# Packing of a gated delta-rule attention kernel: two sequences per partition set with quarter-array products, in place of three sequences with whole-array products

## What is computed

```python
h = tok(x)                                   # 16 x 37 x 256
q, k, v = silu(causal_conv4(h @ Wq)), ...    # 8 heads, key 128, value 64
q, k = l2norm(q), l2norm(k)
beta = 2 * sigmoid(h @ Wb); alpha = exp(-exp(A_log) * softplus(h @ Wa + dt_bias))
state = alpha * (state - beta * (state k) k^T) + beta * v k^T     # for each token
o = state q
o = o * rsqrt(mean(o^2) + 1e-5) * o_norm_w * silu(h @ Wg)
h = layernorm(h + o @ Wo)
h = layernorm(h + int8_linear(h) + bias)
```

## Time and profile before

| | us |
|---|---|
| median of 3 runs | 252.26 |
| profiled execution, span from first to last instruction | 249.4 |
| PE busy | 212.5 (85%) |
| weight loads busy | 175.9 (71%) |
| DVE busy | 183.3 (73%) |
| ACT busy | 91.5 (37%) |
| POOL busy | 57.5 (23%) |

### The profile page before, as it was taken

How to read it: one execution, slowest core, us unless ns; L and a number is a source line. 1 busy time by engine, 2 the same in 40 slices (tenths; PEclk the granted TensorE clock), 3 DMA queues, 4 the chain that set the end, 5 groups by cost and what they waited for, 6 DMA issues and landing times.

```text
span 249.4 us, 3855 instructions
## 1 busy us (share of the span) xinstructions
PE 212.5 (85%) x1292; PEld 175.9 (71%) x1292; DVE 183.3 (73%) x393; ACT 91.5 (37%) x168; POOL 57.5 (23%) x65
## 2 busy tenths in 40 slices
PE   8999897929978999999699999777989999995430
PEld 3767566917856899797489979566868989983320
DVE  0136358999789969799995979989999851355692
ACT  2017883343261554224645422340621123103911
POOL 9100002330000033306003330600260080043541
PEclk9999798895997999989999999977999999999655
DMA  6991110010010001001000000000000000000004
GB/s 222 362 353 47 42 63 0 1 45 0 1 50 13 3 0 45 1 0 42 24 0 0 0 0 0 0 0 0 0 1 4 0 3 0 3 0 1 0 0 106
DMA packets 5682, 8.93 MB, mean 36 GB/s; under 512 B 1251, under 2 KB 3299, under 8 KB 5539
## 3 DMA queue, kind: packets, MB, share of 16 engines
q1 hardware_dynamic: 5075, 8.65, 10.6%
q10 hardware_dynamic: 592, 0.10, 0.3%
HBM read 8.09 MB, written 0.66 MB: 35 GB/s over the span
## 4 chain that ended last, share of the span: by engine, by line
PE 60%; DVE 22%; issue 9%; POOL 3%; ACT 2%; DVEq 1%; POOLq 0%; ACTq 0%
PE PYV L1349 13%; PE PA L1218 12%; PE PS L1311 8%; PE PS L1334 6%; DVE conv L722 5%; PE PA L1197 2%; PE PS L1197 2%; PE PA L1374 2%; DVE tmp L862 2%; PE PYV L1287 2%; DVE xg L804 2%; PE PR L1374 2%; DVE tri L867 1%; POOL x_sb L444 1%; DVE EMs L813 1%
## 5 line engine op out<-in xcount | busy, mean ns | idle before, releaser
L722 DVE SCALAR_TENSOR_TENSOR conv<-xp,tap_sb,conv 128x640 f32<-128x640 f32 x60 | 55.6, 938 | 8.3 <-ACT conv L483 6.7
L402 POOL TENSOR_TENSOR EMs<-Xf,cst 120x640 f32<-120x640 f32 x8 | 15.7, 1961 | 108.3 <-DVE Xf L794 90.3
L1349 PE MATMUL PYV<-y,ZPs 120*120 120x64 f32 x288 | 33.7, 269 | 0.0
L1349 PEld LDWEIGHTS PYV<-y,ZPs 120*120 120x120 f32 x288 | 31.9, 185 | 0.5 <-issue 0.4
L474 ACT ACTIVATE xp<-PA 128x296 f32<-128x296 f32 x40 | 16.0, 416 | 39.9 <-PE PA L1218 39.9
L898 DVE TENSOR_TENSOR y<-R,PYV 120x384 f32<-120x384 f32 x24 | 13.2, 549 | 13.6 <-PE PYV L1349 13.6
L410 POOL TENSOR_TENSOR onrm<-omean,mhalf_c 120x6 f32<-120x6 f32 x8 | 11.6, 1452 | 45.8 <-DVE omean L919 45.8
L1218 PE MATMUL PA<-hT,wq_sb 128*128 128x296 f32 x64 | 21.2, 476 | 0.7 <-ACT xp L474 0.7
L1218 PE MATMUL PA<-hT,wk_sb 128*128 128x296 f32 x64 | 20.3, 449 | 0.9 <-ACT conv L483 0.9
L1218 PEld LDWEIGHTS PA<-hT,wq_sb 128*128 128x128 f32 x64 | 13.3, 221 | 5.3 <-issue 3.2
L1334 PE MATMUL PS<-EMs,T 120*120 120x240 f32 x72 | 16.8, 374 | 0.0
(11 more groups left out here) (156 smaller groups left out, 394.9 us busy)
## 6 DMA issues: line engine op xcount, KB each, us to landing
x_sb<-xT SPq DMA_DIRECT2D x6, 288.0 KB, 3.9
cst<-consts SPq DMA_DIRECT2D x1, 1149.0 KB, 8.7
wk_sb<-wk SPq DMA_DIRECT2D x4, 256.0 KB, 2.6
wq_sb<-wq SPq DMA_DIRECT2D x4, 256.0 KB, 2.6
wlin_sb<-wlin SPq DMA_DIRECT2D x6, 128.0 KB, 4.3
wv_sb<-wv SPq DMA_DIRECT2D x4, 128.0 KB, 2.3
wg_sb<-wg SPq DMA_DIRECT2D x1, 512.0 KB, 9.6
wo_sb<-wo SPq DMA_DIRECT2D x1, 512.0 KB, 10.1
```

The costliest lines, as they stand in the source:

```text
L402: gp.tensor_tensor(EM[h][:, 0, 0:NT], Xf[h][:, :], mask_e, ALU.mult).then_inc(et_made, 1)
L722: dve.scalar_tensor_tensor(conv[c][:, 0:NT], xp[c][:, j:j + NT], tap_sb[:, bass.ds(w * (5 * KS) + c * KS + j, 1)], conv[c][:, 0:NT], ALU.m ...
L1349: mm = pe.matmul(PY[h][0:TT, n * VD:(n + 1) * VD], ZP[h][:, n, 1 if j == NB - 1 else 0, :], y[h][:, n, :] if j else R[:, n, h, :], start=T ...
```

## The change

- **Packing.** Two sequences share a partition set: one on partitions 0 to 39, one on 64 to 103 (`SEAT = 64`, `ROWS = 104`); 8 such sets (`NCP`). No padded tokens between sequences elsewhere: 592 tokens instead of 640.
- **Compact scores.** For each sequence and head one product of 40 x 80 gives both k.k and q.k (`KQ` holds k and q side by side). A head's scores are one PSUM region of 8 x 80 columns, and one DVE instruction (`decayed`, 104 x 640) multiplies them by the decay. The two masks are applied by POOL (`own_block`, `off_diagonal`), one of them was DVE's.
- **Quarter-array matmuls.** `scores`, `zp`, `solve`, `replicate` and the norms of q are now one product for each sequence (40 weight columns, 64 or 80 moving columns; 488 for `replicate`, 1 for the norms), whose operands and results stand in the lower or the upper half of the partitions, the two halves taking turns. Before they were one product for each tile of three sequences.
- **Gate feature-major.** `gates` has the gate weights as stationary operand (4 products of 296 columns instead of 12), and the gate is multiplied in after `o_trans` (`gated`), which also takes the place of the copy `copy_ot` on ACT.
- **Pairs written out.** No hardware loop is left, and every pair has the same order. All weights of the four pairs are loaded at the start, into tiles of their own; the patches are loaded and projected in two halves.
- **Tail of 5 tiles** of up to 128 token rows, 3 and 2 in a group, instead of 6 of 120.

The core of the diff:

```diff
-            def scores(k, v, u):
...
-                for n, cols, off in tiles_of(half):
-                    mm = pe.matmul(PS[k % 2][0:TT, off:off + cols], kT[h][:, n * TT:(n + 1) * TT],
-                                   (kT, qT)[q][h][:, n * TT:n * TT + cols], start=True, stop=True)
+            def scores(h, v):
...
+                for n in range(NCP):
+                    for s in range(2):
+                        mm = pe.matmul(PSN[s * SEAT:s * SEAT + TP, n, 0:2 * TP], KQ[h][:, 2 * n + s, 0, :],
+                                       KQ[h][:, 2 * n + s, :, :].rearrange("p x t -> p (x t)"), start=True, stop=True)
...
-                for n in range(NTILE):
-                    mm = pe.matmul(PY[h][0:TT, n * VD:(n + 1) * VD], ZP[h][:, n, 1 if j == NB - 1 else 0, :],
-                                   y[h][:, n, :] if j else R[:, n, h, :], start=True, stop=True)
+                for n in range(NCP):
+                    for s in range(2):
+                        r = slice(s * SEAT, s * SEAT + TP)
+                        mm = pe.matmul(PY[r, h, n * VD:(n + 1) * VD], ZP[h][r, n, at:at + TP],
+                                       y[h][r, n, :] if j else R[r, n, h, :], start=True, stop=True)
...
+            for u in range(NPAIR):
+                v, w = u + 1, u + 2
+                zp(0, u)
+                if v < NPAIR:
+                    spread_alpha(0, v)
+                    spread_alpha(1, v)
+                if w < NPAIR:
+                    project(0, w)
+                zp(1, u)
+                solve(0, 0, u)
+                solve(1, 0, u)
+                if v < NPAIR:
+                    scores(0, v)
+                if w < NPAIR:
+                    project(1, w)
+                solve(0, 1, u)
+                if v < NPAIR:
+                    scores(1, v)
+                solve(1, 1, u)
+                if w < NPAIR:
+                    project(2, w)
+                solve(0, 2, u)
+                if v < NPAIR:
+                    q_norm(0, v)
+                    q_norm(1, v)
+                solve(1, 2, u)
+                if w < NPAIR:
+                    project(3, w)
+                solve(0, 3, u)
+                solve(1, 3, u)
+                if v < NPAIR:
+                    replicate(0, v)
+                    replicate(1, v)
+                gates(u)
+                if v < NPAIR:
+                    v_trans(v)
+                if w < NPAIR:
+                    project(4, w)
+                if v == NPAIR:
+                    pe.wait_ge(wo_ready, 1)
+                    for n in range(NT):
+                        attn_out(n, range(u))
+                o_trans(u)
```

In the new DVE order of a pair the substitution stands behind `spread`, one tap of component 1 and both `rhs`; o_norm, q_norm and the three taps of component 2 stand between its steps:

```diff
+                    scaled_block(v)
+                    spread(0, v)
+                    spread(1, v)
+                    sub_start(v)
+                    if w < NPAIR: tap(1, 3, w)
+                    rhs(0, v)
+                    rhs(1, v)
+                    for m in range(BL - 1, 0, -1):
+                        sub_product(m, v)
...
+                    sub_end(v)
+                    expand(0, v)
+                    expand(1, v)
...
+                gated(u)
+                if w < NPAIR:
+                    taps(3, w)
```

More of the change, by code:

```diff
@@ L656, in _ @@
-            for half in range(2):
-                copy_ot(half, v)
+                if v < NPAIR:
+                    silu(4, v)
+                if w < NPAIR:
+                    copy_xp(0, w)
+                    tap0(0, w)
+                    copy_xp(1, w)
+                    tap0(1, w)
+                    silu(0, w)
+                    copy_xp(2, w)
+                    tap0(2, w)
+                    silu(1, w)
+                    square_q(0, w)
+                    copy_xp(3, w)
+                    tap0(3, w)
@@ new lines, in _ @@
+            taps(0, 0)
+            softplus_max()
+            softplus_sum()
+            taps(1, 0)
+            make_beta()
+            dve.wait_ge(cst_loaded, 16)
+            scan(0, 0)
+            scan(1, 0)
+            taps(2, 0)
+            decayed(0, 0)
+            taps(3, 0)
+            decayed(1, 0)
+            taps(4, 0)
+            block_scales(0)
+            scaled_block(0)
+            spread(0, 0)
+            spread(1, 0)
+            taps(0, 1)
+            sub_start(0)
@@ L1026, in out_weights @@
+            rhs(0, 0)
+            rhs(1, 0)
+            for m in range(BL - 1, 0, -1):
+                sub_product(m, 0)
+                if m == 6: q_norm(0)
+                if m == 9: tap(1, 1, 1)
+                if m == 8: tap(1, 2, 1)
+                if m == 7: tap(1, 3, 1)
+                sub_difference(m, 0)
+            split_alpha()
+            sub_end(0)
+            expand(0, 0)
+            expand(1, 0)
+            taps(2, 1)
+            taps(3, 1)
             def out_weights():
@@ new lines, in project @@
+            def project(c, w):
+                wt, landed, h = w_of[c]
+                pe.wait_ge(landed[w], 16)
+                for half in range(2):
+                    take(half, xp_copied, 10 * w + 2 * c + half + 1)
+                    for k in range(DC):
+                        mm = pe.matmul(PA[:, half, 0:HTOK], wt[:, w, k, h * KD:(h + 1) * KD],
+                                       hT[:, k, half * HTOK:(half + 1) * HTOK], start=(k == 0), stop=(k == DC - 1))
+                    mm.then_inc(proj_done, 1)
@@ L1366, in attn_out, with o_trans @@
+                mm.then_inc(solve_done, 1)
+            def o_trans(u):
+                pe.wait_ge(ogn_made, 2 * u + 2)
+                for half in range(2):
+                    take(half, ot_made, u + 1)
+                    for n in range(half * NCP // 2, (half + 1) * NCP // 2):
+                        mm = pe.transpose(PAN[:, n, 0:ROWS], ogn[:, n, :, :].rearrange("p h v -> p (h v)"), cst[0:ROWS, C_ID:C_ID + ROWS])
+                    mm.then_inc(otrans_done, 1)
             def attn_out(n, pairs):
+                t = slice(n * P, n * P + rows_of(n))
+                last = n % 2 == 1 or n == NT - 1
@@ L1413, in _ @@
[L1413 to L1431 removed]
+                    mm = pe.matmul(PX[n], OT[:, k, t], wo_sb[:, k, :], start=False, stop=(k == NPAIR - 1 and last))
@@ new lines, in attn_out @@
+                return mm
+            pe.wait_ge(small_loaded, 16 * 5)
+            read[:] = [(h_step, 7), (h_step, 9)]
+            project(0, 0)
+            alpha_of()
+            project(1, 0)
+            beta_of()
+            project(2, 0)
+            project(3, 0)
+            pe.wait_ge(cst_loaded, 16)
+            pe.wait_ge(sel_loaded, 16)
+            pe.wait_ge(alpha_act, 5)
+            spread_alpha(0, 0)
+            spread_alpha(1, 0)
+            project(4, 0)
+            scores(0, 0)
@@ new lines, in _ @@
+            project(0, 1)
+            scores(1, 0)
+            project(1, 1)
+            q_norm(0, 0)
+            q_norm(1, 0)
+            v_trans(0)
+            replicate(0, 0)
+            replicate(1, 0)
+            project(2, 1)
+            project(3, 1)
+            project(4, 1)
+            pe.wait_ge(parts_step, 7)
+            for u in range(NPAIR):
+                v, w = u + 1, u + 2
+                zp(0, u)
+                if v < NPAIR:
+                    spread_alpha(0, v)
[3 more added lines that the diff above has]
+                zp(1, u)
+                solve(0, 0, u)
```

1620 lines of the change are left out of this document (630 added, 990 removed).

## The result

The changed kernel takes 259.4 us (median of four runs, 258.99 to 260.25), the kernel before 252.5 in the same session (251.81 to 253.35): a ratio of 1.027, 95% interval 1.024 to 1.031. It is slower by 2.7%, where 266 us and 5% were forecast. The profiled execution took 259.83 us, with a span of 257.7. Some executions of a kernel take some per cent longer than the rest; the medians count them, and the ratios leave them out.

What follows compares the result with a forecast made beforehand. PE and DVE were taken as both nearly full, PE a little fuller. Start 67, steps 53, 52 and 41, last pair 29 and tail 21.3 sum to 263.3; with 2.9 outside the span, 266 us, range 245 to 292.

Steps and rivals of the forecast that it cites:

- start to first T0: From kernel start to the end of the first expand: 67 us, was 76.9, as DVE's list loses some 9.
- steps: First two: PE 32.3, waits 9.0, DVE 11.0, taken as 53 and 52 us; third, without projections: 41.
- last pair to statistics: Last pair to the first statistics: 29 us, was 27.3, with the output product now behind the solves.
- The three waits that the prediction placed: PE idle within a step: replicate for DVE's spread 2.4 us; gates for ACT's copy and v_trans for the gate's silu, 2.0 together.
- Narrow products: Quarter-array products on PE: 448 records a step at 40 ns each, 17.9 us.
- the lower end: Lowest price of a narrow record: both array halves stream side by side and the weight load binds, 40 ns.
- the halves go one after another: Rival: array halves stream in turn, records cost 54, 67 and 40 ns, 293 us in all; chance 0.20.
- The 2.0 for ACT's zp copies: Wait in each step: ACT's zp copies stand behind silu and square of component 3, which wait for DVE's taps; 2.0 us.
- DVE's stretch: DVE's serial part of a step, substitution with rhs, taps and o_norm, added to PE's part: 11.0 us.
- the savings listed: DVE per step: mask to POOL, shorter scans, gather, taps and fewer score passes; 38.5 becomes about 32 to 33 us.
- the clock falls: Rival: PE's clock is 1.2 GHz through narrow products, doubling wide work and streaming; above 300 us, chance 0.07.
- The faster rival: Rival: waits are not there, a step is 43.3 us, 238 us in all (236 to 249); chance 0.21.

Runs made afterwards that it cites:

- run 2: Run 1 plus rhs moved into DVE's substitution and ACT's copies of o ahead of the silu of component 1 and the gate: 245.5 us, ratio 0.974.
- run 1: Changed kernel with ACT's copy of projection 3 and its tap0 ahead of the silu of component 1 and the square of q: 253.2 us, ratio 1.001.
- run 4: Changed kernel with each solve's lower-half products all first, then the upper-half ones, instead of taking turns: 285.9 us, ratio 1.132.
- run 6: Changed kernel with ACT's four zp copies ahead of the silu of component 3 and the square of the second q: 259.6 us, ratio 1.029.
- run 5: Changed kernel with the last pair's gates ahead of its solves, and the gate's silu behind ACT's zp copies: 254.4 us, ratio 1.009.
- run 7: Changed kernel with moves of runs 1, 2 (rhs earlier) and 6, and gates ahead of the solves in third step and last pair: 230.5 us, ratio 0.911.
- run 11: Run 7 with the silu of component 2 behind ACT's copy of projection 4, and products of zeros on PE behind o_trans: 229.5 us, ratio 0.910.
- run 12: Run 5 with unused whole-array products added in the last pair's solves, between narrow products (head 0) or behind them (head 1): 269.1 us.

## Why the prediction was right, and where it was off

| | forecast | measured |
|---|---|---|
| start to first T0 | 67 | 63.7 |
| steps | 53, 52, 41 | 49.1, 47.9, 43.0 |
| last pair to statistics | 29 | 33.6 |
| tail | 21.3 | 20.4 |
| outside the span | 2.9 | 2.1 |

**The structure held.** Both engines less busy and the step longer, because PE's stretch and DVE's stretch stand one after the other: run 2 took 14 us off by moving nothing but what the substitution waits for, with all products, DVE operations and packing in place. Run 2 contains the move of run 1, and part of what the two gave back was clock, so the 14 us are order and what order does to the clock. The three waits that the prediction placed (replicate for spread, the gates for the copy behind the silu of component 1, rhs for v_trans behind the gates) stand in the timeline where it put them.

**Narrow products: too dear.** A record of a solve takes 28 ns, not 40. From start to start the narrow groups of the first step add up to 14.1 us, changes of mode included, where 17.9 and 1.1 were taken. The term that was mis-sized is the lower end, which let the weight load bind at 40 ns. The pace is nearer to half of the stream: 28 against half of 54 for 64 columns, and (1.30 - 0.22) / 31 = 35 in zp against half of 67 for 80. The load does not show in it; whether it is shorter than the 34 ns taken or lies under the other half's stream, no row tells. That the halves go one after another (293 us) is refuted by run 4. A mode change was taken at 0.1 us and costs 0.14, so the 11 of a step are 1.5 of the 14.1 us.

**Waits: too many.** PE is idle 1.4, 1.2 and 1.6 us between T0 and v_trans in the first step, 4.2 where 6.4 were taken besides clock and mode changes. The 1.4 ahead of projection 0, for ACT's copy of a projection, were not among those placed. The 2.0 for ACT's zp copies were wrong in the first two steps, where projection 0 covers them, and in the third run 6 shows that taking them away gives nothing.

**DVE's stretch** was taken at 11.0; from the end of v_trans (101.0) to T0 (112.8) it is 11.8. Two of the taps in it took 1.56 and 1.44 us instead of 0.83, 1.3 us more together, both beside POOL's o_scale (104.62 and 107.87). DVE's total was taken too low: the savings listed add up to 7.2, which gives 31.3 and not 32 to 33, and the first two steps had 34.7 and 32.9.

**Clock: sized too small, most of all at the end.** In the first step spread_alpha (1.3), projection 0 (4.2) and the gates (3.6 to the next start) ran at half clock, 4.1 us above 0.75, 2.15 and 2.1; the forecast had 1.5. With that the step is 52.3 - 3.8 (narrow) - 1.1 (modes) - 2.2 (waits) + 2.6 (clock) + 0.8 (DVE) + 0.3 (wide work at full clock) = 48.9, against 49.1: products and waits too dear by 7.1, clock too cheap by 2.6. In the third step and the last pair less cancelled. The forecast had let the clock fall behind idle time only and had put 1.0 us on it, with solves that ran at 1.00 before as its ground; but those were whole-array records behind wide products. Now zp, all eight solves and the gates of the last pair ran at half clock, and run 5, 5 us faster with a last pair of 27.7 us, accounts for all of the 4.6 us by which that stage was missed. The rival "the clock falls" (0.07, above 300 us) had the mechanism right and its extent wrong: by the granted clocks of 0.66 and 0.68, about two thirds of the third step and of the last pair, not all narrow work of the kernel.

**The faster rival** named waits below about 4.4 us as the point where it decides. These waits include the clock's cost: the first step had 4.2 of idle time and 4.1 of clock, 8.3 in all before any mode change, so the rival's condition was not met. Runs 2 and 7, at 245.5 and 230.5 us, are that rival made true by order.

**Start, and what is luck.** The start came 3.3 us early: DVE's busy time fell by 9.4 us (46.5 to 37.1) as taken, and its idle time from 14.4 to 10.6, which nothing here explains (76.9 less 9 is also 68, not 67). The 2.9 outside the span set a median against another execution's span; run by run the kernel before has 1.8 (251.91 and 250.1). That 266 lies within 3% of 259.4 owes something to errors that cancel: in the first step 7.1 us too dear against 3.7 too cheap, and over the kernel start and first two steps 11 us too long, third step and last pair 7 too short.

## What to carry to other kernels

When a change makes two engines' work cheaper, look at what one does while the other runs its serial chain: here 9 us of cover shrank to 2 ahead of o_trans, and another order of the same work took off 14 us, and 29 with all moves. Price an idle gap on PE at more than its length, since the products behind it can run at half clock, and try a wide product that has to be done anyway ahead of a run of narrow ones. Move products away from behind the last solve only if others still cover the engine that is waited for.

## What the hardware showed that was not expected

- PE that was busy without a gap stayed at a granted clock of 0.50 for 18 us of quarter-array products (203.75 to 221.9), and behind 4.07 us of wide f32 products it was 1.00. The same quarter-array products, begun at 1.00, kept it for 7.6 us in run 5; in the third step of the changed kernel it fell at about 181.1 among them, without a gap.
- Gates behind 1.6 us of idle PE took 3.79 us, without it 2.26 (run 1). With fillers up to them zp, spread_alpha and projection 0 took 1.30, 0.75 and 2.16 us (run 11, second step) instead of 2.35, 1.31 and 3.88 in the changed kernel.
- Two halves of the array with weights of 40 columns, taking turns: 28 ns a record at full clock and 53 at half ((10.45 - 0.31) / 191), 51 apart at full clock. A change of tiling mode: 0.14 us.
- In run 12 the granted clock fell from 1.00 (214.2 to 222.2) to 0.50 (from 222.3) although PE was busy throughout; what set it off there stays open.
- A tap of 592 columns takes DVE 0.83 us, and 1.56 and 1.44 when it stands beside POOL's o_scale (104 x 512, 1.04 us). A tap of the kernel before took 1.51 us instead of 0.89 in such a place (117.07). No run moves either of them, so the cause is not shown.
